# Orders of two slots, the last unit and the last program's head, and attention weights turned by VectorE and placed by DMA

## The reference

```python
x = x + jnp.tanh(g_xattn[0]) * _L0_xattn_ref(_layernorm(x), ctx_4096, ctx_4096, mask, wq, wk, wv, wo, 0)
x = x + jnp.tanh(g_ffn[0]) * _L0_ffn_ref(_layernorm(x), Wg, Wu, Wd)
x = x + jnp.tanh(g_xattn[1]) * _L1_xattn_ref(_layernorm(x), ctx_4096, Wq, bq, Wk, bk, Wv, bv)
x = x + jnp.tanh(g_ffn[1]) * _L1_ffn_ref(_layernorm(x), W_base, b_base, lora_A, lora_B, router_W, router_b, domain_prior, active)
```

## Time and profile before

| | us |
|---|---|
| median of three runs | 765.0 |
| lowest and highest | 763.45, 765.17 |
| profiled execution | 764.38 |
| its span | 762.2 |
| TensorE busy (share of the span) | 741.7 (97%) |
| VectorE busy | 590.0 (77%) |
| GpSimd busy | 511.7 (67%) |
| ScalarE busy | 491.7 (65%) |
| mean granted TensorE clock (1 is full speed) | 0.996 |

### The profile page before, as it was taken

How to read it: one execution, slowest core, us unless ns; L and a number is a source line. 1 busy time by engine, 2 the same in 40 slices (tenths; PEclk the granted TensorE clock), 3 DMA queues, 4 the chain that set the end, 5 groups by cost and what they waited for, 6 DMA issues and landing times.

```text
span 762.2 us, 13617 instructions
## 1 busy us (share of the span) xinstructions
PE 741.7 (97%) x4789; PEld 591.2 (78%) x4806; DVE 590.0 (77%) x1131; ACT 491.7 (65%) x1084; POOL 511.7 (67%) x439
## 2 busy tenths in 40 slices
PE   8999899999999999999999999999889999999998
PEld 7877688888888888888888888777546777787776
DVE  5888888777888776677776666777899997898873
ACT  5755666665667545655564655447689898888773
POOL 2678777756657865556885547757787877787752
PEclk9999999999999999999999999999999999999999
DMA  9310463333453122341213300156344333122101
GB/s 337 122 69 29 112 158 84 111 90 105 120 122 94 52 98 75 80 140 56 70 46 102 85 2 28 44 219 238 83 111 106 90 93 89 37 62 64 49 15 42
DMA packets 66192, 71.10 MB, mean 93 GB/s; under 512 B 39965, under 2 KB 41469, under 8 KB 65613
## 3 DMA queue, kind: packets, MB, share of 16 engines
q1 hardware_dynamic: 65836, 69.90, 32.1%
q10 hardware_dynamic: 288, 0.33, 0.1%
HBM read 49.12 MB, written 6.34 MB: 73 GB/s over the span
## 4 chain that ended last, share of the span: by engine, by line
PE 85%; DVE 6%; ACT 4%; POOL 3%; issue 2%; DMA 1%; SPq 0%; DVEq 0%; ACTq 0%
PE bank L81 12%; PE bank L83 11%; PE bank L82 11%; PE bank L589 7%; PE bank L597 7%; PE bank L590 7%; PE bank L662 4%; PE bank L1852 4%; PE bank L571 4%; PE bank L1838 4%; PE bank L1806 2%; PE bank L1785 2%; PE bank L1777 2%; PE bank L1828 2%; PE bank L1829 2%
## 5 line engine op out<-in xcount | busy, mean ns | idle before, releaser
L1370 POOL TENSOR_TENSOR rope_swap<-rope_swap,trig 128x512 f32<-128x512 f32 x80 | 105.3, 1316 | 131.7 <-ACT rope_swap L754 131.5
L1068 DVE SCALAR_TENSOR_TENSOR x_res<-bank,gate,x_res 128x512 f32<-128x512 f32 x124 | 92.1, 744 | 53.5 <-PE bank L597 53.2
L885 ACT CAST oT_hi<-bank 128x512 fp32r<-128x512 f32 x64 | 34.4, 589 | 108.4 <-PE bank L662 108.3
L589 PE MATMUL bank<-wo_hi,oT_hi 128*128 128x512 f32 x256 | 100.6, 393 | 2.4 <-DVE x_res L1068 1.2
L81 PE MATMUL bank<-xnT_hi,wq_hi 128*128 128x512 f32 x252 | 102.0, 405 | 0.0
L83 PE MATMUL bank<-xnT_hi,wq_lo 128*128 128x512 f32 x252 | 100.4, 399 | 0.0
L590 PE MATMUL bank<-wo_lo,oT_hi 128*128 128x512 f32 x256 | 100.1, 391 | 0.0
L82 PE MATMUL bank<-xnT_lo,wq_hi 128*128 128x512 f32 x252 | 100.0, 397 | 0.0
L1376 POOL TENSOR_TENSOR q_rope<-rope_cos,rope_swap 128x512 f32<-128x512 f32 x64 | 82.9, 1295 | 5.0
L3196 POOL TENSOR_TENSOR b_e<-b_e,b_inv 128x512 f32<-128x512 f32 x64 | 68.3, 1080 | 18.9 <-DVE b_inv L2382 18.4
L597 PE MATMUL bank<-wo_hi,oT_lo 128*128 128x512 f32 x256 | 78.9, 391 | 0.0
(11 more groups left out here) (272 smaller groups left out, 1959.9 us busy)
## 6 DMA issues: line engine op xcount, KB each, us to landing
wq_raw<-in_wq_tiles SPq DMA_DIRECT2D x16, 512.0 KB, 3.7
wo_raw<-in_L_xattn_wo SPq DMA_DIRECT2D x16, 512.0 KB, 4.1
xn<-in_L_ffn_Wd SPq DMA_DIRECT2D x16, 256.0 KB, 2.8
b_ctx<-in_ctx SPq DMA_DIRECT2D x32, 128.0 KB, 2.7
b_k_twice<-b_qk_hi SPq DMA_DIRECT2D x32, 128.0 KB, 2.4
w_T_dram<-w_out SPq DMA_DIRECT2D x28, 128.0 KB, 3.0
w_T<-w_T_dram SPq DMA_DIRECT2D x2, 1376.0 KB, 9.1
xn<-in_L_ffn_Wg SPq DMA_DIRECT2D x10, 256.0 KB, 4.0
```

Of the source, the lines that this page charges most:

```text
L589: pe.matmul(out, oT_hi[:, tl, h], wo_hi[jp][:, h, :], start=(h == 0), stop=False)
L1068: dve.scalar_tensor_tensor(out=K.x[:, t, :], in0=wo_ps[t % 2][:, :], scalar=K.gate[:, 0:1], in1=K.x[:, t, :], op0=ALU.mult, op1=ALU.add).t ...
L1370: pool.tensor_tensor(out=sw, in0=sw, in1=sin_b, op=ALU.mult).then_inc(s_rope, 1)
```

## The change

Five things change.

- **Slot 1.** ScalarE swaps the row sums of unit 2 before it evacuates the slot's second projection.
- **Slot 29.** VectorE's accumulation of the next unit's tile 4 moves from the head of the last slots in front of the slot's second cosine; ScalarE's copy of the wo weights goes behind its second evacuation.
- **Last unit.** TensorE does `values` of unit 31 before `low_b_select`, and `logit_T` moves from the head of the last program to between `low_b_select` and `output_pair(31)`. ScalarE does `attended(31)` before `low_b_hi`.
- **Head of the last program.** The lists of all four engines are reordered up to tile 0's last row maxima: `x_transpose(0)` before the third output tile, the fourth output tile later, the exponents and row maxima of tile 0 earlier, the late statistics later.
- **Turned weights.** For units n = 0 and 4 of tiles 1 to 6, twelve units in all, `weights_T` and `copy_T` are gone. VectorE turns the 128x512 weights in blocks of 32x32 into `b_turned`, SP stores that into one of two buffers in DRAM and, once it has landed, reads it back in four DMAs, one for each 32 partitions of `b_eT`, in pieces of 128 floats. The rows of a block come out in another order, which the store's layout and another slice of the weights in `attend` take up. The semaphores of the first program's pieces are used again.

```diff
@@ last_slots, tensor @@
                 output(U - 1, (2, 3))
+                values(g, 1, 1, U)
                 low_b_select()
-                values(g, 1, 1, U)
+                logit_T()
                 output_pair(U)
@@ first_slots, scalar @@
                 exp_unit(2)
+                swap_halves(2, SUM_OWN)
                 evacuate(*items1[1])
-                swap_halves(2, SUM_OWN)
@@ body, scalar @@
-                    if not (last and jp == 1):
+                    if not (last and jp == 1) and U != 2 * NPAIR - 3:
                         wo_piece(2 * g + jp + 1, u)
                     for G, pos in items[1:]:
                         evacuate(G, pos)
+                    if U == 2 * NPAIR - 3:
+                        wo_piece(2 * g + jp + 1, u)
@@ last_slots, scalar @@
+                attended(U)
                 low_b_hi()
-                attended(U)
@@ slot, vector @@
+                if U == 2 * NPAIR - 3:
+                    accumulate(UT * U, 4)
                 if late(U):
                     for G, pos in items[1:]:
                         cosine(G, pos)
@@ last_slots, vector @@
-                accumulate(before, 4)
@@ last_programs @@
+    TURNED = [NB * t + n for t in range(1, NT - 1) for n in (0, 4)]
@@ attend, tensor @@
-                pe.wait_ge(s_eT_sb, NB * t + 2 * tb + 2)
+                pe.wait_ge(s_eT_sb, by_pe(NB * t + 2 * tb + 2))
+                if is_turned(NB * t + 2 * tb):
+                    pe.wait_ge(L0.s_p_T, L0.n_p_T + 64 * turned_before(NB * t + 2 * tb + 2))
@@ the list of the last program, tensor: its head @@
-            first.logit_T()
+            x_transpose(0)
             first.output(2 * NPAIR - 1, 2)
-            x_transpose(0)
-            first.output(2 * NPAIR - 1, 3)
             logits(0, 0)
             gate_mm(0, 0)
             up_mm(0, 0)
+            logits(0, 1)
             qk(1, 0)
-            logits(0, 1)
+            first.output(2 * NPAIR - 1, 3)
@@ the same, further on: one of twelve @@
-            weights_T(1, 0)
@@ new, vector @@
+            def turn_weights(t, n):
+                m = NB * t + n
+                k = turned_before(m)
+                dve.wait_ge(s_w, m + 1)
+                if k:
+                    dve.wait_ge(L0.s_p_out, L0.n_p_out + 16 * k)
+                dve.transpose(M.turned[:, :].rearrange("p (q c i) -> p c q i", q=4, c=DC),
+                              e[m % 4][:, :].rearrange("p (c q i) -> p c q i", c=DC, q=4)).then_inc(L0.s_probT, 1)
@@ exps, scalar @@
-                after(act, s_eT, m - 3)
+                if m >= 4 and is_turned(m - 4):
+                    act.wait_ge(L0.s_probT, L0.n_turned + turned_before(m - 3))
+                else:
+                    after(act, s_eT, by_pe(m - 3))
@@ new, sync @@
+            def place_weights(t, n):
+                k, tb = turned_before(NB * t + n), n // 2
+                sp.wait_ge(L0.s_probT, L0.n_turned + k + 1)
+                if k > 1:
+                    sp.wait_ge(L0.s_p_T, L0.n_p_T + 64 * (k - 1))
+                sp.dma_start(K.turned_dram[k % 2], M.turned[:, :]).then_inc(L0.s_p_out, 16)
+                sp.wait_ge(s_av, 4 * (t - 1) + tb + 1)
+                sp.wait_ge(L0.s_p_out, L0.n_p_out + 16 * (k + 1))
+                blocks = K.turned_dram[k % 2].rearrange("(a j) (q n) -> q j a n", a=4, q=4)
+                for q in range(4):
+                    rows = slice(q * P // 4, (q + 1) * P // 4)
+                    sp.dma_start(eT[0][rows, :, tb * P:(tb + 1) * P], blocks[q]).then_inc(L0.s_p_T, 16)
```

More of the change, by code:

```diff
@@ L226, in n_out @@
             return sum(16 * (2 if i[4] % P else 1) for k, i in enumerate(whole) if k % 2 == b)
+        shared.s_probT, shared.s_p_T, shared.s_p_out = s_probT, s_p_T[0], s_p_out[0]
+        shared.n_turned, shared.n_p_T = 2 * NPAIR, 16 * ((n_quant(len(PIECES)) + 1) // 2)
+        shared.n_p_out = n_out(n_quant(len(PIECES)), 0)
+        tail = last_programs(cx, K, M, K.W, K.W1, shared, ctx_dram, out_dram)
         def column(p):
@@ L698, in _ @@
             first = Keep()
-            first.output, first.logit_T = output_tile, logit_T
+            first.output = output_tile
             tail.tensor(pe, first)
@@ L1626, in late_buffers @@
     M.ctx_split = two("b_ctx_split", [P, D], F32R)
+    M.logit_row = take("l1_logit_row", [P, E_ACT])
+    assert late.used <= at["q_rope1"]
     late.used = at["q_rope1"]
@@ L1634, in late_buffers @@
     M.low_w = take("l1_low", [P, DC, P + E_ACT])
-    M.logit_row = take("l1_logit_row", [P, E_ACT])
+    M.turned, late.used = Area(cx.nc, K.late_base + late.used, 4 * D).take("b_turned", [P, D]), late.used
     M.spread = take("l1_spread", [E_ALL, P])
@@ L1696, in last_programs, with is_turned, turned_before, by_pe @@
     programs = Keep()
+    TURNED = [NB * t + n for t in range(1, NT - 1) for n in (0, 4)]
+    def is_turned(m):
+        return m in TURNED
+    def turned_before(m):
+        return sum(i < m for i in TURNED)
+    def by_pe(m):
+        return m - turned_before(m)
     if True:
@@ L1835, in weights_T @@
                     pe.wait_ge(M.s_w_low, 1)
-                after(pe, s_eT_sb, m)
+                after(pe, s_eT_sb, by_pe(m))
                 for c in range(DC):
@@ L1851, in attend @@
                         ch = slice(par * S, (par + 1) * S)
-                        mm = pe.matmul(av_of(t, tb)[ch, cols], v[:, c, ch], eT[par][:, c, cols], start=(c == 0), stop=(c == DC - 1))
+                        weights = eT[par][:, c, cols]
+                        if par == 0 and is_turned(NB * t + 2 * tb):
+                            weights = eT[par][:, :, tb * P + c * P // 4:tb * P + (c + 1) * P // 4]
+                        mm = pe.matmul(av_of(t, tb)[ch, cols], v[:, c, ch], weights, start=(c == 0), stop=(c == DC - 1))
                 mm.then_inc(s_av, 1)
@@ L1923, in tensor @@
             logits(0, 2)
+            pe.wait_ge(s_qk_lo[0], 2)
+            qk(1, 1)
             pe.wait_ge(s_gate, 2)
@@ L2487, in vector @@
             first.statistics((1, 2, 3))
+            row_max(0, 0)
+            first.shift(slice(1, UT), 2)
             scale_gate(0, 0)
-            first.shift(slice(1, UT), 2)
             scale_up(0, 0)
-            row_max(0, 0)
+            row_max(0, 1)
             lo_qk(1, 0)
@@ L2494, in vector @@
             front(1)
+            scale_up(0, 1)
+            row_max(0, 2)
             make_h(0, 0)
-            scale_up(0, 1)
-            row_max(0, 1)
-            row_max(0, 2)
             lo_qk(1, 1)
@@ L2508, in vector @@
             make_h(0, 1)
+            late_statistics(0)
             row_max(0, 5)
@@ L2535, in vector @@
             scale_gate(2, 0)
+            turn_weights(1, 0)
             shift_of(0)
@@ L2553, in vector @@
             row_max(1, 7)
+            turn_weights(1, 4)
             x3_shift_of(0)
@@ L2572, in vector @@
             row_max(2, 3)
+            turn_weights(2, 0)
             route_end(0)
@@ L2605, in vector @@
             residual(2)
+            turn_weights(3, 0)
             row_max(3, 3)
@@ L2619, in vector @@
             scale_gate(4, 1)
+            turn_weights(3, 4)
             lo_qk(5, 1)
@@ L2636, in vector @@
             make_h(4, 1)
+            turn_weights(4, 0)
             make_h(4, 2)
@@ L2651, in vector @@
             lo_qk(6, 0)
+            turn_weights(4, 4)
             output(4)
@@ L2668, in vector @@
             row_max(5, 4)
+            turn_weights(5, 0)
             scale_up(6, 0)
@@ L2682, in vector @@
             residual(4)
+            turn_weights(5, 4)
             row_max(5, 7)
@@ L2715, in vector @@
             row_max(6, 6)
+            turn_weights(6, 4)
             make_h(7, 0)
@@ L2890, in scalar @@
             first.late_copy(2)
+            exps(0, 0)
+            x_normalise(1)
+            tanh_half(0, 0)
             hi_qk(1, 0)
-            x_normalise(1)
+            exps(0, 1)
             first.late_copy(3)
-            tanh_half(0, 0)
-            exps(0, 0)
+            x_shifted(1)
             tanh_half(0, 1)
-            x_shifted(1)
+            exps(0, 2)
             hi_qk(1, 1)
             split_hi(2, 1)
-            exps(0, 1)
-            exps(0, 2)
             first.low_part()
-            tanh_half(0, 2)
             xT_copy(1)
             exps(0, 3)
+            tanh_half(0, 2)
             copy_T(0, 0)
@@ L3008, in scalar @@
             xT_copy(4)
-            copy_T(3, 0)
             exps(3, 3)
@@ L3236, in gpsimd @@
             late_add(2)
+            product(0, 0)
             late_add(3)
-            product(0, 0)
             product(0, 1)
@@ L3435, in sync @@
             load_ctx(5, 1)
+            place_weights(1, 0)
             duplicate(3, 1)
+            place_weights(1, 4)
             load_ctx(5, 0)
             duplicate(3, 0)
+            place_weights(2, 0)
             duplicate(4, 0)
             load_ctx(6, 0)
+            place_weights(2, 4)
             store(0)
@@ L3443, in sync @@
```

(9 more changed lines are left out.)

32 lines of the change are left out of this document (4 added, 28 removed).

## The result

The changed kernel takes 768.2 us, median of 6 runs (766.6 to 769.1), where the kernel before, run beside it, takes 765.1 (763.5 to 765.9): ratio 1.0045, 95% interval 1.0035 to 1.0056, so 3.4 us slower (2.7 to 4.3). Forecast was 761.2, faster. The profiled execution has a span of 766.8 us against 762.2.

A forecast was written before the change was run, and what follows sets the result against it. TensorE, busy 741.7 of 762.2 us, was taken as the bound, VectorE next. Terms -3.5 - 0.4 + 3.1 - 3.0 = -3.8 us gave 760.6 against the profiled 764.4, 761.2 against the median; range 756.5 to 768.3.

The forecast's parts named there:

- Slot 1: Row sums first on ScalarE: TensorE's gap of 2.90 us becomes 1.1 and the clock stays up; -3.5 us, bounds -1.8 and -3.5.
- leaves the clock up: the other 1.7 us: Slot 1: behind a gap of only 1.1 us the clock does not fall, which gains 1.7 us besides 1.8.
- Slot 29: Earlier accumulation of tile 4 ends a 0.86 us wait, rope gains 0.37 us; -0.4 us, bounds 0 and -1.3.
- Last unit and head: Logit transpose waits for l_spread 4.6 us, low clock and later waits follow; +3.1 us, bounds -2 and +5.
- VectorE, full from here to 608, carries that on: Head of last program: the first weights transpose starts 3.1 us late, and full VectorE carries that loss on to 608 us.
- Turned weights: Tiles 1 to 6: twelve units leave TensorE, 5.3 us, less 0.9 and 1.4; -3.0 us, bounds -5.3 and +2.4.
- about a third of the gain, 1.4 us, goes into waits: Ten turned units in 608 to 722 us: VectorE at 96% makes TensorE give back 1.4 us.
- VectorE as the bound: Turned weights cost +2.4 instead of -3.0, with one clock-lowering stall of 1.7 us: 768.3 us; chance 0.17.
- The placed weights: Loads land late, so fifth units of tiles 1, 2 and 3 each hold TensorE about 1.5 us: 765.7 us; chance 0.13.
- Slot 1's clock: In slot 1 the clock falls anyway behind the shortened gap: 762.9 us; chance 0.14.
- The head: The last program's head doesn't lose, because something ahead of l_spread is earlier than read: 758.1 us; chance 0.11.
- signs for "wrong": Attention matmuls waiting on DMA, gate or logit matmuls on VectorE over 2 us in sum, or no wait before logit transpose.

The follow-up runs named there:

- run 3: Kernel before with only the last unit's and the head's new orders up to tile 1, no turned weights: 770.19 us, ratio 1.0066.
- run 5: Kernel before with the last unit's and head's new orders, but the logit transpose put back behind the last unit's first two output tiles: 765.6 us, ratio 1.0002.
- run 10: Kernel before with slot 1's swap and only five turned units (both of tiles 4 and 5, first of tile 6): 760.94 us, ratio 0.995.
- run 4: Kernel before with only the twelve turned weights, store and loads included, head as before: 764.57 us, ratio 0.9993.
- run 12: Kernel before with the twelve turned weights and VectorE's transposes, but without their store and loads (old values read): 763.8 us, ratio 0.9992.
- run 9: Changed kernel with VectorE's router offset moved to right behind slot 31's last turn: 764.94 us, ratio 1.0003 against the kernel before.
- run 11: Changed kernel with VectorE's router offset moved earlier and only five units turned: 762.51 us, ratio 0.997 against the kernel before.
- run 6: Kernel before with only the last unit changed: values before selection, then the logit transpose, then four output tiles: 769.64 us, ratio 1.0059.
- run 7: Kernel before with the twelve units' TensorE transposes removed, and no VectorE transposes, store or loads instead (old values read): 761.8 us, ratio 0.9952.
- run 1: Kernel before with only slot 1's swap of the row sums ahead of the evacuation on ScalarE: 762.69 us, ratio 0.9976.

## Why the prediction was wrong, step by step

*Slot 1, -3.5 forecast, -1.8 measured.* Gap (1.13 us) and clock (1.00) came as forecast. The failing step is "leaves the clock up: the other 1.7 us": it took TensorE's gain of speed for a gain of time, and didn't ask which engine comes second in the next 10 us. VectorE did, held by GpSimd for 0.7 us besides: 0.55 us of wait at 85.8, and smaller pieces behind. That -1.8 is also the bound I gave for a falling clock is chance; the clock did not fall.

*Slot 29, -0.4 forecast, -0.2 measured*: nothing that can be told apart.

*Last unit and head, +3.1 forecast, +5.1 measured.* The mechanism and nearly all its times were right: a wait of 4.2 us (forecast 4.6) for l_spread, twelve matmuls at the low clock, a second gap of 1.0 us, waits before the second x transpose and the first weights transpose; 563.8 was forecast for the latter, 563.99 was it in run 3. The sum ended there. The step that failed is the one behind it, "VectorE, full from here to 608, carries that on": it took the 3.1 us as passed on unchanged. But I priced the two last gaps as waits and not as gaps that take the clock down again (1.7 us), and left out the waits behind them (in run 3 0.44 us for b_eT and 0.90 us for f_h, which in the kernel before are 0.16 and 0.36). That is most of the way from the 3.3 us at 563.99 to the 6.0 at 577.09. The 0.90 us stands in run 5 too, so it belongs to the orders of the head. +5.1 lies just past my upper bound of +5.

*Turned weights, -3.0 forecast, -0.5 measured.* The term that was mis-sized is the give-back, "about a third of the gain, 1.4 us, goes into waits". I had it from VectorE's occupancy of the stretch; its busy time there came nearly true (103.00 us against 104.7), but the waits follow from the place of each transpose in the queue, not from the mean. In tiles 1 to 3, and again in front of b_z, a transpose stands before what TensorE wants next, and together they cost what they gain; in tiles 4 and 5 no new wait follows. Nor was the price of 0.64 us for each right: the twelfth cost VectorE 1.2 us, the five of run 10 together 1.0. The bounds, -5.3 and +2.4, held. The Trainium skill's advice against VectorE for a 128x128 transpose ("VectorE: DVE Perf Modes", "Rules for kernel authors") is borne out for the twelve (run 4, -0.5 us) and not for the five (run 10); the measurement decides. The round trip by DMA was free for the twelve (run 12), and in run 10 no wait of TensorE is for a DMA.

*The rivals.* VectorE as the bound was the nearest in direction and place, but it made the turned part worth nothing, not the loss of 2.4 us that this rival has, and from 570 to 722 us the clock stays at 1.00; that its time, 768.3, is that of the measurement is luck. The placed weights were never late: no wait of TensorE on them, and run 12. Slot 1's clock did not fall. The head did lose. What I had no case for is that three terms fall short together, by 1.7, 2.0 and 2.5 us (with 0.2 of slot 29 6.4 of the 7.2 us between -3.8 and +3.4; the other 0.8 stay open): all my errors had the same sign, because each gain was priced on TensorE and the cover it ran into only in the turned part.

*The signs.* The gap in slot 1 and the clock behind it showed as written; the logit wait was 3.81 us, a little under the 4 to 5, the clock behind it 0.50, and the gap of 2.83 us is gone (the longest behind it up to tile 0's attention is 1.90). There are 52 groups of weight transposes, and VectorE is at 90.4% from 608 us. Of the signs for "wrong" none appeared as worded: I had looked for VectorE's waits at the gate and logit matmuls, and they came at v_item, the base matmuls and the z transpose, 2.2 us, with 1.2 us more through ScalarE's b_xn.

## What to carry to other kernels

A small instruction on the engine that feeds all others must never wait for one of them in front of that feed: 4 us of TensorE's wait became 6 us of idleness on three engines, so that nothing behind could make up for it, and the low clock came on top. When a gap of the bound engine is closed, look for who is second over the next 10 us before counting the clock's gain. And work moved to a nearly full engine is to be placed unit by unit, in front of nothing that the bound engine wants next: five of twelve units gave 2 us, all twelve 0.5. What it costs there is not its own length: look also at which instruction of the neighbour it pushes the next ones onto, or off.

## What the runs showed of the hardware

- The clock also fell behind two short gaps close together, but not each time. 1.89 and 1.35 us, 0.9 us of work between them, were followed by 0.57 for 4.0 us (run 3) and by 0.52 for 6.1 us (run 5), and 1.90 and 1.18 us by 0.50 for 4.3 us (the changed kernel); in runs 9 and 11 nearly the same pair was followed by 1.00. The lone gaps of 1.1 us in slot 1 were followed by 1.00 in every profile. A longer gap need not bring it down either: behind 2.64 us in run 6 (to 562.40) the clock was 1.00 until 566, where behind 2.83 us it is 0.54 in the earlier trace rows.
- The same gap cost different amounts from one execution to the next. Behind slot 1's 2.90 us the clock from 79 to 85 us was 0.72 in seven profiles and 0.50 in those of runs 4 and 7, which were then 1.3 us later in all that followed. A difference of that size between two single profiles says nothing of the kernels.
- Two engines that had passed each other by 0.16 us collided once one of them came earlier (run 1: 0.69 us became 1.38). A saved microsecond can shift VectorE onto a GpSimd instruction that it used to follow, and an added one can do so too (the twelfth turned unit: 1.04 became 1.67) or take it off one (run 10: 1.20 became 0.51).
- VectorE's transpose of 128x512 took 0.70 us in all twelve places, also at 599.04, where four loads of 32 rows each, issued from 597.67, were under way; the stores and loads through DRAM, 2.0 us to land as a median, held up nobody.
